# A table of edge places for the fixed one-hots of a graph-network kernel, and their turn in two rounds

## The reference, cut to what matters

```python
summed = jax.ops.segment_sum(msg, dst, num_segments=n_nodes)              # SAGE, rounds 1 to 3
agg = jax.ops.segment_sum(message, dst, num_segments=x.shape[0])          # GIN, round 4
agg = jax.ops.segment_sum(xw[row] * norm[:, None], col, num_segments=n)   # GCN, rounds 5 and 6
agg = jax.ops.segment_sum(h_rel[etype, src], dst, num_segments=h.shape[0])  # relational, rounds 7 and 8
```

## Time and profile before

| | |
|---|---|
| median of three runs | 5383.45 us (5371.6 to 5387.2) |
| the profiled execution | 5378.48 us |
| its span, first to last instruction | 5376.4 us |
| PE busy | 4387.9 us, 82% of the span |
| DVE busy | 3446.8 us, 64% |
| ACT busy | 2416.5 us, 45% |
| POOL busy | 1921.9 us, 36% |
| DVE, line L1566, all compares | 1126.1 us, 2848 of them |
| PE waited for one-hots | 344.6 us before L1132 and 109.1 us before L1129 |

### The profile page before, as it was taken

The page is one execution under the profiler, slowest core; times in us unless marked ns, Lnnn a source line. Parts: engine busy times, 40 slices in busy tenths (PEclk is TensorE's granted clock), DMA queues, the critical chain, the costliest instruction groups (busy, mean ns, idle before and its releaser), DMA issues.

```text
span 5376.4 us, 129953 instructions
## 1 busy us (share of the span) xinstructions
PE 4387.9 (82%) x25128; PEld 2875.8 (53%) x25129; DVE 3446.8 (64%) x10510; ACT 2416.5 (45%) x4969; POOL 1921.9 (36%) x1886
## 2 busy tenths in 40 slices
PE   6998997777878888867777688887799996888895
PEld 4664554433445555535554355543577773677672
DVE  5553454787545555449997688876566663777774
ACT  2442442555257777526664466664222211333332
POOL 5650782654033333016550443310433312333310
PEclk9999999899889999989999899998899999999997
DMA  4663884665234444325553466653444433443432
GB/s 142 217 210 117 260 270 149 195 192 174 90 122 147 149 146 145 111 96 171 174 172 103 145 210 205 211 173 109 137 136 137 140 116 109 129 130 125 128 100 76
DMA packets 443919, 815.61 MB, mean 152 GB/s; under 512 B 70872, under 2 KB 76818, under 8 KB 443828
## 3 DMA queue, kind: packets, MB, share of 16 engines
q1 hardware_dynamic: 389172, 697.28, 38.4%
q0 software_dynamic: 54656, 117.32, 8.9%
HBM read 480.10 MB, written 334.22 MB: 151 GB/s over the span
## 4 chain that ended last, share of the span: by engine, by line
PE 46%; issue 15%; DVE 14%; DVEq 8%; ACT 7%; POOL 5%; DMA 3%; ACTq 2%; SPq 1%; POOLq 0%
PE p_agg L1132 8%; PE p_edge L1119 7%; PE p_agg L1134 7%; PE p_tr L1119 6%; POOL raw L696 4%; PE p_agg L1165 4%; DVE onehot L1566 4%; DVE stats L1658 3%; ACT u L916 2%; PE p_wide L1252 2%; ACT o L897 2%; DVEq L373 2%; PE p_agg L1158 2%; DVEq L1566 2%; PE p_dense L1208 2%
## 5 line engine op out<-in xcount | busy, mean ns | idle before, releaser
L1566 DVE TENSOR_SCALAR onehot<-iota,dst_f,negbase 128x512 f16<-128x512 f16 (+1 forms) x2848 | 1126.1, 449 | 815.6 <-PE p_agg L1165 305.3
L1132 PE MATMUL p_agg<-onehot,msg 128*128 128x512 f16 (+1 forms) x2848 | 1138.3, 400 | 596.5 <-DVE onehot L1566 338.6
L696 POOL DMA_INDIRECT raw<-node_s,src_i x980 | 958.7, 978 | 1449.1 <-DMA node_s<-o 561.4
L1134 PE MATMUL p_agg<-onehot,msg 128*128 128x512 f16 (+1 forms) x2848 | 1140.3, 400 | 0.0
L1132 PEld LDWEIGHTS p_agg<-onehot,msg 128*128 x2848 | 281.8, 99 | 941.4 <-issue 791.1
L696 POOL DMA_INDIRECT raw<-node_x,src_i x392 | 378.8, 966 | 551.0 <-DMA feature<-more_masked 253.6
L897 ACT ACTIVATE o<-v_ring,nmr,rstd 128x128 f32 (+1 forms) x1176 | 472.5, 482 | 76.6 <-DVE nmr L1674 71.5
L1165 PE MATMUL p_agg<-h_in,w 128*128 128x512 f32 x784 | 443.3, 649 | 22.9 <-DMA h_in<-feature 21.9
L1658 DVE BATCH_NORM_STATS2 stats<-v_ring 128x6 f32 (+1 forms) x1960 | 417.7, 278 | 44.3 <-DVE v_ring L1647 15.9
L916 ACT ACTIVATE u<-v_ring,nmr,rstd 128x128 f32 (+1 forms) x784 | 312.5, 481 | 225.0 <-DVE res_in L1704 134.7
L1134 PEld LDWEIGHTS p_agg<-onehot,msg 128*128 x2848 | 282.7, 99 | 219.1 <-issue 32.0
(11 more groups left out here) (260 smaller groups left out, 7741.9 us busy)
## 6 DMA issues: line engine op xcount, KB each, us to landing
node_s<-o SPq DMA_DIRECT2D x392, 256.0 KB
h_in<-feature SPq DMA_DIRECT2D x392, 256.0 KB
feature<-u SPq DMA_DIRECT2D x294, 256.0 KB
node_x<-o SPq DMA_DIRECT2D x294, 256.0 KB
res_in<-node_x SPq DMA_DIRECT2D x294, 256.0 KB
h_in<-node_s SPq DMA_DIRECT2D x196, 256.0 KB
h_t<-dinv_scratch SPq DMA_DIRECT2D x196, 256.0 KB
h_in<-in_x SPq DMA_DIRECT2D x98, 256.0 KB
```

The lines of the kernel that those rows point to most:

```text
L696: nc.gpsimd.indirect_dma_start(out=raw[:, (e % RING) * BATCH + j, :], out_offset=None, in_=src_d, in_offset=bass.IndirectOffsetOnAxis(ap=s ...
L1132: nc.tensor.matmul(p_agg[:, a, :], tile_ap(msg, t, 0, D), oh, start=first, stop=True, skip_group_check=True)
L1134: return nc.tensor.matmul(p_agg[:, a, :], tile_ap(msg, t, D, 2 * D), oh, start=False, stop=True, skip_group_check=True)
L1566: return V.tensor_scalar(tile_ap(onehot, slot), iota[:, :], dst_f[:, bass.ds(t, 1)], negbase[:, bass.ds(it * 2 + a, 1)], ALU.subtract, ALU ...
```

## The change

In the first round, after the three fixed compares of a half, DVE writes their three places, `dst_f + negbase`, into a new table `place` (128 x 294). In rounds 2 to 8 the fixed compares read the table: `iota` is compared with one column, whose number follows from the half alone. In the two GCN rounds (`k` of 4 and 5, the fifth and the sixth) the fixed one-hots of half (it+1, 0) are moved to the top of the step, ahead of the list load and of the groups of half (it, 1). Elsewhere their turn stays.

```diff
+        place = sb("place", [P, NHALF * EVERY])
...
-                def first_onehots(it, a, t0):
+                def placed_onehots(it, a):
                     if k:
                         wait(dve, q.out_done, it * 2 + (a - 1))
                     elif rel:
                         wait(dve, q.turned, it * 2 + (a - 1))
                     for j in range(EVERY):
+                        last = V.tensor_scalar(tile_ap(onehot, EVERY * a + j), iota[:, :],
+                                               place[:, bass.ds((it * 2 + a) * EVERY + j, 1)], None, ALU.is_equal)
+                    last.then_inc(q.every_ready.semaphore, 1)
+
+                def first_onehots(it, a, t0):
+
+                    if r:
+                        placed_onehots(it, a)
+                        return
+                    for j in range(EVERY):
                         last = compare(it, a, EVERY * a + j, (t0 + j).with_bounds(min_val=0, max_val=TILES - 1))
                     last.then_inc(q.every_ready.semaphore, 1)
+                    V.tensor_scalar(place[:, bass.ds((it * 2 + a) * EVERY, EVERY)],
+                                    dst_f[:, bass.ds(t0.with_bounds(min_val=0, max_val=TILES - EVERY), EVERY)],
+                                    negbase[:, bass.ds(it * 2 + a, 1)], None, ALU.add)
...
                 def onehots(it, these):
-                    if not rel:
+                    if not rel and k < 4:
                         first_onehots(it, 0, these[0])
                     more_onehots(it, 0, these)
...
                 def first_gcn_step(it):
+                    if exists(it + 1):
+                        placed_onehots(it + 1, 0)
                     now, after, ahead = next_items(it)
...
                 def second_gcn_step(it):
+                    if exists(it + 1):
+                        placed_onehots(it + 1, 0)
                     now, after, ahead = next_items(it)
```

## The result

The changed kernel takes 5339.09 us (median of four runs, 5332.68 to 5341.71) against 5379.42 us of the kernel before in the same comparison: a ratio of 0.9927, with a 95% interval of 0.9911 to 0.9942. That is 40 us less, where 80 were forecast; the range held it, the size was off by half. The profiled execution took 5332.68 us, its span 5330.5.

The account below looks back on a forecast made before the run. No engine was taken to fill rounds 3, 5 and 6, where DVE's step sets the pace; PE bounds round 1. Terms -28 - 26 - 12 - 15 + 1 = -80 from 5378.5 gave 5298 us, range 5240 to 5350.

Parts of the forecast that it names:

- The column: Fixed compares: reading one column instead of two saves 0.06 us a compare, 0.18 us a triple.
- The rival in which it costs nothing: Fixed compares: dropping a column saves nothing, so the gain is 49 us and the time 5329; chance 0.15.
- Round 1: First round: 98 small table writes on DVE, hidden behind PE's 461 us of work; +1 us, upper end +34.
- Rounds 4, 7 and 8: Forecast with round 2 at nothing: PE's 88 waits for one-hots end 0.25 us earlier, two thirds reaching the end; -15 us.
- Round 6: Sixth round: 0.65 us a step saved by move, column and dropped register instructions, in about 43 regular steps; -28 us.
- After the move the compares follow the low parts without the gap: Sixth round, DVE: the idle 0.87 us ahead of the first compare goes once the first triple precedes the list load.
- the sum at 3414.4: Sixth round: the move brings the sum out of PSUM from 3414.79 to 3414.4, 0.35 us a step.
- a sign of being wrong: Sixth round: the forecast is wrong if the gap shows again ahead of the sum at its full 0.87 us.
- Round 5: Fifth round: the moved triple escapes POOL's multiplication, 1.85 us saved in three steps, 14 times; -26 us, bounds -10 and -50.
- the third gains 0.35 + 0.18: Fifth round: of three steps, the one meeting no POOL multiplication gains 0.35 us by the move and 0.18 by the column.
- something else ends last: Rounds 3, 5 and 6: ACT, PE or a gather ends last, only 0.2 us a step arrive; 5349, chance 0.12.
- Round 3: Third round, without the move: 0.55 us a step, half taken because POOL blocks some; -12 us, bounds 0 and -25.

## Where the prediction was right and where it failed

- **The column** was right: 60 ns measured for 0.06 forecast, 0.26 us apart. The rival in which it costs nothing falls: 408 and 348 ns differ by the column alone, since one column with two operations takes 348 too. With it falls, as far as it has no term for columns, the rule of the Trainium skill, page "VectorE: DVE Perf Modes", section "The TRN2 errata — SBUF-src ops pay a fixed extra latency per instruction".
- **Round 1** was right: its 98 writes of 222 ns left it at 470.7 us.
- **The error by rounds.** By the two profiled executions the change gained 46 us of 80. Of the 34 that are missing 23 lie in rounds 4, 7 and 8 and 11 each in rounds 5 and 6; rounds 1 to 3 gave 11 more than forecast.
- **Rounds 4, 7 and 8** failed at the step "88 waits of PE for a one-hot, 0.25 us earlier each, two thirds of it reaching the end": -15 forecast, +8 measured. Next to none of it reached the end: rounds 4 and 7 changed by 1.2 and 2.4 us, less than they vary between runs, and with the old compares round 7 is no longer and round 4 some 2 us at most. In round 8 the waits moved to the loads, and at the lower clock, for which the sum had no term, PE's busy time in the regular steps grew by 12.7 us. I had asked who waits for the one-hot, not what PE would wait for next.
- **Round 6**, -17 for -28. The step's gain was nearly right, (424.4 - 406.8) / 30 = 0.59 us for 0.65 (the kernel before took 424.4 us for these 30 steps), but not its parts and not the count. "After the move the compares follow the low parts without the gap" held, and "the sum at 3414.4" did not: the gap shows again ahead of the sum at its full 0.87 us, which the prediction had named as a sign of being wrong. From the low parts to the sum the sequencer never rests: 3.00 us before, 2.75 with the move and without it, 2.73 with the load first, and 3.57 with a second load (medians). Moving engine work out of its way shortens nothing there; only fewer register instructions do. The move itself gave 2.4 us over 30 steps, 0.08 a step and not 0.35. By the run with two columns (412.9 us for the 30 steps) the column gave 0.20 a step, and the dropped register instructions have the rest, 0.30, if the parts add. And the forecast counted 43 regular steps. The 30 gave 17.6 us and the nine ahead of them 2.2; the 11 late ones, which I had set aside as not regular, lost 3.3 us by the move and took 1.9 more than before.
- **Round 5**, -15 for -26. The long triples went, as forecast, the low parts are as long as before (11 of about 3 us in either profile), and the step of the triples gave 1.1 us for 1.3. But "the third gains 0.35 + 0.18" failed, the other two steps gave 0.1 and 0.2 (by their list loads; before, the 30 steps took 323.2 us, so three gained 14.0 / 10 = 1.4 us for 1.85), and the late steps lost 5.2 us by the move. The fixed compares shrank from the 126.8 us of the earlier trace rows to 96.5 and the idle time ahead of them from 27.5 to 1.3, 56.5 us in all; the waits that follow on DVE grew by 20.9 us ahead of the sum and 17.1 ahead of the statistics. By line, before and after (count, busy, mean, then idle time):

```profile
L1685 DVE TENSOR_TENSOR agg_t<-p_agg,h_t 128x512 f32<-128x512 f32 x98 | 66.9, 682 | 20.1 <-PE p_agg L1158 20.0
L1658 DVE BATCH_NORM_STATS2 stats<-v_ring 128x6 f32 (+1 forms) x392 | 81.5, 275 | 7.0 <-ACT v_ring L905 6.8
```
```profile
L1577 DVE TENSOR_SCALAR onehot<-iota,place 128x512 f16<-128x512 f16 x294 | 96.5, 384 | 1.3 <-DVE bt L1904 1.0 <-issue 0.4
L1699 DVE TENSOR_TENSOR agg_t<-p_agg,h_t 128x512 f32<-128x512 f32 x98 | 67.3, 687 | 41.0 <-PE p_agg L1159 34.7 <-issue 6.3
L1672 DVE BATCH_NORM_STATS2 stats<-v_ring 128x6 f32 (+1 forms) x392 | 82.6, 277 | 24.1 <-ACT v_ring L906 24.0
```

  That is the rival "something else ends last", true in kind of round 5 alone, where 14.0 / 30 = 0.47 us a step arrived and not the rival's 0.2; I had given it to all three rounds or to none.
- **Round 3**, -20 for -12: the low parts came out of POOL's multiplication, where I had taken half. Their 28 took 49.4 us before and 30.7 after:

```profile
L1561 DVE TENSOR_TENSOR msg<-raw,msg x28 | 49.4, 1764 | 21.6 <-ACT msg L821 15.6 <-issue 5.9
```
```profile
L1562 DVE TENSOR_TENSOR msg<-raw,msg x28 | 30.7, 1095 | 22.4 <-ACT msg L822 16.3 <-issue 6.1
```

  With two columns they are back at 52.4 us and the round at 573.0, so this belongs to the 60 ns. That so small a saving shifted the phase between the engines is how I read it; no run tests the phase alone.
- **Two sums of the prediction** do not come out, and neither bears on the outcome. The low end of 5244 needs 10 us more than its terms give: with round 5 at -50, round 3 at -25 and all 22 us of the 88 waits it is 5254. And the rival without a column's cost keeps 0.47 us a step in round 6 although the 0.35 had "the operand of this triple included"; without it 0.29 a step are left, 12 us, and the rival stands at 5337.

What stays open: whether the lower clock follows from the length of PE's waits or from something that goes with it. The runs changed the arrival, not the wait alone, and the length of a single wait does not settle it: with the old compares in round 8 the clock fell twice in the regular steps though no wait was longer than 2.0 us, and with the idle writes it fell at one of three waits of 2.1 to 2.3 us.

## What to carry to other kernels

Ask of each saving not only who waits for it but what that engine waits for next: a wait that only changes its name is worth nothing, and one that grows on TensorE can cost more than it saved. Where a gap is ended by "issue", count the register instructions and loads of the whole stretch; their order is worth little, while a second list load in 48 steps cost 33.8 us. And price the irregular steps by themselves: the same move gained 8.7 us in the regular steps and lost 8.5 in the others.

## What the hardware showed

A column as scalar operand costs 60 ns a compare of 128x512 and a second operation nothing measurable. Work added to DVE made the changed kernel faster: 98 pairs of idle writes took 12.7 us off the eighth round. With them TensorE's longest wait in the regular steps was 2.3 us instead of 3.1, and its granted clock 1.00 instead of 0.97.
